# Small-head attentions: each stack of query and key pieces moved for 16 heads in one transfer, 18 transfers per batch in place of 36

## What is computed

```python
x = x + _L0_attn_a_ref(_layernorm(x), ...)   # here kind "norm": q and k get a layernorm over their 8 channels, no mask
x = x + _L0_ffn_ref(_layernorm(x), ...)      # six layers of local attention and MLP, run twice
x = x + _L0_attn_b_ref(_layernorm(x), ...)   # kind "latent": q, k, v through 32 latent channels, causal
...
x = x + _L1_attn_b_ref(_layernorm(x), ...)   # kind "plain": causal

logits = einsum('bhsd,bhtd->bhst', q, k) / sqrt(8)
att = softmax(logits)
out = einsum('bhst,bhtd->bhsd', att, v)      # then the 16 heads side by side, times a 128 x 128 matrix
```

## Time and profile before

| | |
|---|---|
| median of 3 runs | 4770.1 us (4769.83 to 4776.0) |
| the profiled execution | 4769.9 us, of which the span shown is 4768.1 us |
| PE busy | 4283.0 us (90%) |
| DVE, ACT, POOL busy | 3412.0, 2775.9, 2327.6 us |
| attention "norm" | about 35 to 375 us of the span |
| attention "latent" | about 2135 to 2430 us |
| attention "plain" | about 4398 to 4685 us |

### The profile page before, as it was taken

The page is one execution under the profiler, slowest core; times in us unless marked ns, Lnnn a source line. Parts: engine busy times, 40 slices in busy tenths (PEclk is TensorE's granted clock), DMA queues, the critical chain, the costliest instruction groups (busy, mean ns, idle before and its releaser), DMA issues. The chain is left out here.

```text
span 4768.1 us, 129948 instructions
## 1 busy us (share of the span) xinstructions
PE 4283.0 (90%) x54312; PEld 2101.0 (44%) x54312; DVE 3412.0 (72%) x5204; ACT 2775.9 (58%) x6997; POOL 2327.6 (49%) x1448
## 2 busy tenths in 40 slices
PE   5897999999999999976879999999999999877688
PEld 2222544544454544432434444454544444433343
DVE  3773888888888888853548888888888888733463
ACT  2664666666666666642546666666666666543354
POOL 3102766666666666642006666666666666500200
PEclk8998999999999999986889999999999999988699
DMA  5212000000000000003310000000000000000320
GB/s 150 32 19 58 2 20 7 2 20 7 20 7 20 7 2 2 2 4 41 41 37 24 2 23 3 20 6 20 7 2 24 2 2 2 2 4 9 49 33 10
DMA packets 87860, 88.62 MB, mean 19 GB/s; under 512 B 36632, under 2 KB 79860, under 8 KB 83444
## 3 DMA queue, kind: packets, MB, share of 16 engines
q1 hardware_dynamic: 86420, 74.11, 7.7%
q10 hardware_dynamic: 864, 6.29, 0.3%
HBM read 44.13 MB, written 7.34 MB: 11 GB/s over the span
## 5 line engine op out<-in xcount | busy, mean ns | idle before, releaser
L422 POOL TENSOR_TENSOR ra<-ra,rb 128x1024 f32<-128x1024 f32 x384 | 924.0, 2406 | 390.9 <-DVE rb L711 388.2
L436 POOL TENSOR_TENSOR qkr<-ra,inv 128x1024 f32<-128x1024 f32 x384 | 731.3, 1904 | 607.0 <-ACT inv L663 602.0
L466 PE MATMUL ps<-wvo,xs 128*32 128x512 f32 x6144 | 821.8, 607 | 72.6 <-ACT vs L599 52.3
L500 PE MATMUL ps<-wq,xs 128*128 128x512 f32 x1536 | 749.9, 611 | 19.5 <-DMA wq<-in_L_ffn_Wqkv 18.6
L641 ACT ACTIVATE pr<-ps,neg 128x64 f32<-128x64 f32 x3072 | 669.9, 338 | 0.6 <-DVE neg L688 0.6
L599 ACT ACTIVATE vs<-ps 128x512 f32<-128x512 f32 x768 | 451.7, 588 | 321.9 <-PE ps L466 320.2
L1428 DVE TENSOR_REDUCE nm<-ps 128x1 f32<-128x512 f32 (+3 forms) x768 | 382.1, 549 | 244.7 <-PE ps L1237 243.7
L688 DVE TENSOR_REDUCE neg<-ps 128x8 f32<-128x512 f32 x384 | 264.4, 688 | 379.7 <-PE ps L522 379.7
L652 ACT ACTIVATE inv<-ssq 128x16 f32<-128x16 f32 x384 | 82.8, 216 | 678.8 <-DVE ssq L746 678.8
L500 PEld LDWEIGHTS ps<-wq,xs 128*128 128x128 f32 x1536 | 273.4, 191 | 443.9 <-issue 352.3
L522 PEld LDWEIGHTS ps<-kt,qt 64*32 64x32 f32 x24576 | 359.5, 107 | 243.8 <-issue 243.8
(11 more groups left out here) (225 smaller groups left out, 6377.1 us busy)
## 6 DMA issues: line engine op xcount, KB each, us to landing
qs<-cut SPq DMA_DIRECT2D x216, 64.0 KB
ks<-cut SPq DMA_DIRECT2D x216, 64.0 KB
wq<-in_L_ffn_Wqkv SPq DMA_DIRECT2D x12, 1024.0 KB, 5.1
wvo<-wvo_scratch SPq DMA_DIRECT2D x12, 1024.0 KB, 4.9
wvo_scratch<-pt ACTq DMA_DIRECT2D x6, 1024.0 KB, 4.1
w<-in_L_ffn_W SPq DMA_DIRECT2D x12, 341.0 KB
pt<-in_L_ffn_Wqkv SPq DMA_DIRECT2D x6, 512.0 KB, 8.4
pt<-in_L_ffn_Wo SPq DMA_DIRECT2D x6, 512.0 KB, 7.7
```

Of the source, the lines that this page charges most:

```text
L422: pool.tensor_tensor(ra[:, m % 2, :, :], ra[:, m % 2, :, :], rb[:, :, :], ALU.add).then_inc(sum_done.sem, 1)
L436: pool.tensor_tensor(qkr[:, m % 2, :, :].rearrange("p s (h c) -> p (s h) c", c=HD), ra[:, m % 2, :, :].rearrange("p s (h c) -> p (s h) c", ...
L466: last = pe.matmul(VP[32 * j:32 * j + 32, :], xs[:, turn % 2, v * WIN:v * WIN + WIN], wvo[:, l % 2, j, :], start=True, stop=True)
L500: last = pe.matmul(PJ[:, qk, :], xs[:, turn % 2, t * P:t * P + P], wq[:, l % 2, at:at + 512], start=True, stop=True)
```

## The change

The order of channels becomes (channel, head) over all 128 partitions, so one DMA takes a piece for all 16 heads: from 128 partitions to 8, 128 KB in place of 64 KB. `ld_low` and `ld_high` become one `ld_stack`, for which PE waits at head 0. The transfers of batches 0 and 1 stand where the lower half stood (k = -15 and k = 1), those of batches 2 and 3 where the upper half stood (k = 16(b-1) + 7), behind the wait that the upper half had. The gamma and beta columns of "norm" are loaded by 4 DMAs in place of 8.

```diff
-        "mean_of_8": np.kron(np.eye(2), np.kron(np.full((SD, SD), 1 / SD), np.eye(SH // 2))).astype(np.float32),
+        "mean_of_8": np.kron(np.full((SD, SD), 1 / SD), np.eye(SH)).astype(np.float32),
...
                     for col, name in enumerate(("q_gamma", "q_beta", "k_gamma", "k_beta")):
-                        for e in range(2):
-                            by_row = d[f"{n}_{name}"][:, None].to_broadcast([SD, SH // 2])
-                            sp.dma_start(gb[P // 2 * e:P // 2 * e + P // 2, col:col + 1], by_row, allow_slow_non_contiguous=True).then_inc(ld_w.sem, 16)
+                        by_row = d[f"{n}_{name}"][:, None].to_broadcast([SD, SH])
+                        sp.dma_start(gb[:, col:col + 1], by_row, allow_slow_non_contiguous=True).then_inc(ld_w.sem, 16)
...
-            by_channel = lambda a: a.rearrange("p s (e c h) -> p s e h c", e=2, c=SD)
-            by_head = lambda a: a.rearrange("p s (e h c) -> p s e h c", e=2, c=SD)
-            n_ld = {"norm": 3 + 8 + 4, "latent": 7 + 4, "plain": 4}[kind]
+            by_channel = lambda a: a.rearrange("p s (c h) -> p s h c", c=SD)
+            by_head = lambda a: a.rearrange("p s (h c) -> p s h c", c=SD)
+            n_ld = {"norm": 3 + 4 + 4, "latent": 7 + 4, "plain": 4}[kind]
...
-            def stacks(b, low):
+            def stacks(b):
 
-                heads = slice(0, SH // 2) if low else slice(SH // 2, SH)
-                half = slice(0, P // 2) if low else slice(P // 2, P)
-                done = ld_low if low else ld_high
                 for part_ in range(PARTS):
                     sp.wait_ge(cut_done.sem, cut_done.at(5 * b + 2 * part_ + 1))
                     for to, s, p, c in [(qs, 0, c // PARTS, c) for c in range(PARTS * PARTS)] + [(ks, 1, c % PARTS, c) for c in range(PARTS * PARTS)]:
                         if p != part_:
                             continue
                         rows = slice(SD * c, SD * c + SD)
-                        sp.dma_start(to[rows, b % 2, heads, :], cut[half, p, s, :]).then_inc(done.sem, 16)
+                        sp.dma_start(to[rows, b % 2, :, :], cut[:, p, s, :]).then_inc(ld_stack.sem, 16)
...
-                if (b := batch_at(k, 1)) is not None:
-                    if b >= 2:
-                        sp.wait_ge(st_mm.sem, st_mm.at(NP * (SH * (b - 2) + SH // 2)))
-                    stacks(b, True)
-                if (b := batch_at(k, 7)) is not None:
+                if (b := batch_at(k, 1 if k < SH else 7)) is not None:
                     if b >= 2:
                         sp.wait_ge(st_mm.sem, st_mm.at(NP * SH * (b - 1)))
-                    stacks(b, False)
+                    stacks(b)
...
                     if b:
-                        pool.wait_ge(ld_low.sem, ld_low.at(16 * loads * b))
-                        pool.wait_ge(ld_high.sem, ld_high.at(16 * loads * b))
+                        pool.wait_ge(ld_stack.sem, ld_stack.at(16 * loads * b))
...
                 if n_ == 0 and h == 0:
-                    pe.wait_ge(ld_low.sem, ld_low.at(16 * loads * (b + 1)))
-                if n_ == 0 and h == SH // 2:
-                    pe.wait_ge(ld_high.sem, ld_high.at(16 * loads * (b + 1)))
+                    pe.wait_ge(ld_stack.sem, ld_stack.at(16 * loads * (b + 1)))
```

More of the change, by code:

```diff
@@ L929, in small_attention @@
     qk_normed, qk_ready, cut_done = ev("sa_qk_normed", "sa_qk_ready", "sa_cut_done")
-    ld_low, ld_high, *ld_m = ev("sa_ld_low", "sa_ld_high", "sa_ld_m_even", "sa_ld_m_odd")
+    ld_stack, *ld_m = ev("sa_ld_stack", "sa_ld_m_even", "sa_ld_m_odd")
     vw_turned, vw_made, vw_kept_act, vw_kept_dve, vw_out_act, vw_out_dve = ev(
@@ L1047, in _ @@
                     dve.tensor_tensor(by_channel(w[:, 0:2, :]), by_head(tmp[:, 0:2, :]),
-                                      mean.rearrange("p s (e h) -> p s e h", e=2)[:, :, :, :, None].to_broadcast([P, 2, 2, SH // 2, SD]), ALU.subtract).then_inc(prep_dve.sem, 1)
+                                      mean[:, :, :, None].to_broadcast([P, 2, SH, SD]), ALU.subtract).then_inc(prep_dve.sem, 1)
                     dve.tensor_copy(w[:, 2, :], tmp[:, 2, :])
@@ L1062, in _ @@
                     dve.wait_ge(prep_pe.sem, prep_pe.at(5))
-                    dve.tensor_copy(by_channel(w[:, 0:2, :]), ps[:, 0, 0:2 * P].rearrange("p (s e h c) -> p s e h c", s=2, e=2, c=SD))
+                    dve.tensor_copy(by_channel(w[:, 0:2, :]), ps[:, 0, 0:2 * P].rearrange("p (s h c) -> p s h c", s=2, c=SD))
                     dve.tensor_copy(w[:, 2, :], ps[:, 0, 2 * P:3 * P])
@@ L1498, in small_attention @@
     ones_set.past(1)
-    for e in (ld_low, ld_high):
-        e.past(16 * loads * BATCH)
+    ld_stack.past(16 * loads * BATCH)
     for e in ld_m:
```

## The result

The changed kernel takes **4969.9 us** (median of 4 runs, 4962.0 to 4972.1) against 4773.1 us (4 runs, 4769.8 to 4779.6) for the kernel before: **1.0408 times** as long, interval 1.039 to 1.0426. That is +197 us where +132 had been forecast: the sign and the mechanism were right, the size was short by a third, and the time lies only just inside the range. The profiled execution took 4962.0 us, its span is 4960.2 us, and against 4768.1 us before the span has grown by 192.1 us.

The account below looks back on a forecast made before the run. PE was taken to wait for maxima behind stack transfers draining by bytes. Later maxima +124.9, cold TensorE +10 and fewer gamma and beta loads -2.5 gave +132 us on 4769.9, so 4902 us; 8-in-10 range 4820 to 4970.

Parts of the forecast that it names:

- What bounds the place: Three small attentions: PE waits for maxima queued behind stack transfers, eleven waits, 79.5 us; bytes bound it, not transfer number.
- L: Time from first issue of a batch's stacks until all 2.36 MB have landed; taken as 36.5 us, bounds 31.1 and 38.0.
- rival 3: Stack sets drain worse than by bytes, at 53 GB/s: L 45.8 us, 5022 us; 4940 to 5030 given chance 0.10.
- Each us of L counts nine times: Batches 1 to 3 of three attentions each pay for L; 31.1 gives 4853 us, 38.0 gives 4916.
- 67 GB/s as the rate of the kernel before: Queued stacks drain at 67 GB/s; 100 GB/s appears in one of the twelve sets only.
- 124.9 as predicted: Later maxima in batches 1 to 3, in us: norm 47.9, latent 37.1, plain 39.9; together 124.9.
- cold TensorE: After a wait for maxima PE runs at a lower clock; five places newly waiting at 2.0 us each: +10.
- the loads of gamma and beta: Preparation of norm: four fewer issues of 0.62 us on SP, -2.5 us, bounds -2.5 and 0.
- The issue time: SP's issue of a batch 1 set still takes 11.8 us; even 23.6 us would cost nothing.
- Head 0's wait in latent: Batch 1: PE waits for the full stack, 17 us later, at no cost, covered by the wait for group 0's maxima.
- 1 (per transfer): Stack queue: 128 KB takes the 0.97 us of 64 KB, L 18.7 us, -68 us, 4702 us; 4700 to 4760 chance 0.08.
- 2 (100 GB/s, held back by issue alone): Stack queue keeps its fast state, 100 GB/s: L 24.9 us, 4769 us; chance 0.04.

Follow-up runs that it names:

- e6: The changed kernel with the three small maxima transfers issued by POOL on its own queue instead of SP's: 4843.9 us, 1.0146 of the kernel before.
- e1: The changed kernel with each stack transfer's 8 target partitions nine apart instead of neighbours: 4696.6 us, 0.9837 of the kernel before.
- e3: The kernel before with both 64 KB stacks put where the changed kernel has its one, transfer size unchanged: 4919.5 us, 1.0298 of the kernel before.
- e8: The changed kernel with its 18 transfers reordered, so 9 of 17 passages stay on the same partitions or those 32 away: 5003.1 us, 1.0478.
- e5: The changed kernel with each transfer's 8 target partitions two apart, the ninth pairing left as neighbours: 4798.5 us, 1.0055 of the kernel before.
- e2: The kernel before, with its 36 transfers of 64 KB, given target partitions nine apart: 4696.3 us, 0.9836 of the kernel before.
- e4: The changed kernel with the three small maxima transfers issued by ACT on its own queue instead of SP's: 4946.0 us, 1.0351 of the kernel before.

## Why the prediction was right in kind and short in size

**What bounds the place: right.** PE waits for the maxima behind the stacks. e6 moves the maxima to another queue and takes 126 us back; e1 leaves them there, makes the stacks drain, and takes back 273.

**L: the term that was mis-sized.** "By bytes, L is 2.36 MB / 67 GB/s" took the rate of the small transfer for that of the large one. Measured are 60 to 61 GB/s in five of the nine sets, 62 to 65 in the other four, and a mean L of 41.1 us. With the small transfers in the same places (e3) the mean L is the 36.5 us of the forecast, and the time 4919.5, 17 above it. So the 36.5 held for 64 KB and failed for 128 KB. Its likely cause was on the table as rival 3: the burst of about 100 GB/s once per transfer belongs to the passage between two transfers, and larger ones have half as many. The quarter-microsecond windows of the changed kernel in "latent":

```profile
2300.50:2300.75 0.25, 0.00 (x0) 0.00 (x0) 0.00 (x0) 0.00 (x0) 0.00 (x0) 0.50 0.54 57
2300.75:2301.00 0.25, 0.00 (x0) 0.00 (x0) 0.00 (x0) 0.00 (x0) 0.00 (x0) 0.50 0.49 78
2301.00:2301.25 0.25, 0.00 (x0) 0.00 (x0) 0.00 (x0) 0.00 (x0) 0.00 (x0) 0.50 0.72 86
2301.25:2301.50 0.25, 0.00 (x0) 0.00 (x0) 0.00 (x0) 0.00 (x0) 0.00 (x0) 0.50 0.55 53
```

This is the only burst among the twelve quarters from 2300 to 2303; before, the twelve from 2216 to 2219 have three, of 98 to 119 GB/s. e8 shows the passage at work. Rival 3 took the 53 GB/s for the whole set and put L at 45.8, as if the larger transfers had no burst at all. With its own mechanism, half as many bursts, the rows give the measured value: 0.97 us for the first 64 KB of a transfer and 64 KB / 53 GB/s = 1.24 us for the second, 18 times 2.21 and 1.3 us, an estimate of 41.0 us. I had given 4940 to 5030 us a chance of 0.10, with the alternation that speaks for it in the rows; it deserved more.

**Each us of L counts nine times: wrong, it counts eleven to twelve.** The forecast let batch 0's set stay as it was ("the same bytes"). But batch 0's set is one of the larger transfers too, and batch 1's cut hangs on its landing. It took 1.6 (norm), 4.7 (latent) and 10.6 us (plain) longer, measured on SP's and POOL's rows: 16.9 us. In plain the slip could be seen beforehand: batch 0's set stayed in the sum at its 31.1 us while every other set was given 36.5. Rival 3 counts the later landing of these sets (36 us), the main sum doesn't. From e5 to the changed kernel the sets of batch 0 grow by 1.6, 14.8 and 14.8 us, 2.2 for each of the 13.9 us of L, so that 11.2 of the 11.6 us are accounted for. The same quotient of the medians is 10.9 from e3 to the changed kernel and 10.7 from there to e8.

**67 GB/s as the rate of the kernel before: a reading that was too narrow.** The prediction held that the trace shows 100 GB/s in one of the twelve sets only. The set of batch 0 in "plain", the one of 31.1 us, drained faster as well. The windows of the kernel before:

```profile
4438.00:4440.00 2.00, 0.62 (x1) 0.00 (x0) 0.00 (x0) 0.60 (x1) 0.00 (x0) 0.50 0.57 90
4440.00:4442.00 2.00, 1.90 (x11) 1.46 (x12) 1.15 (x3) 0.00 (x0) 0.00 (x0) 0.50 0.57 91
```

Batch 1's in norm (79 to 111 GB/s from 114 to 128) and the upper stack of plain's batch 3 (79 to 90 from 4592 to 4604) did too, at a share of 0.54 to 0.60, with 64 KB transfers to neighbouring rows. In e3 the set of batch 0 in plain drains at 72 GB/s on the mean, where it was 82, and takes 35.2 us. So 4.1 of the 10.6 us came without the larger transfer. What lets such a set run faster stays open.

**Sum again.** 124.9 as predicted; 9 places by their own L less 36.5, +41.4; batch 0's sets, +16.9; cold TensorE, +10; the loads of gamma and beta, -4.8 (first stack of norm at 62.65 instead of 67.43, and 62.4 to 65.4 in the other kernels with that edit; predicted -2.5). That is 188.4 us of the 192.1 by which the span grew. With the 4.9 us between the attentions the sum is 1.2 us too large. The + 10 is the forecast's and was seen in two places only (below).

**Parts that held.** The issue time costs nothing: in latent each group of three from the fourth on took SP 3.4 to 7.4 us instead of 1.9, as the queue was full, and what lands last was behind the queue anyway. Head 0's wait in latent (21.64 us, expected 17) was covered as forecast: PE still waits another 25.18 us for the maxima afterwards. In plain it is 25.24 and in norm 9.22. The cold stretch is there: from the landing to the next group's cut 9.5 us (238.76 to 248.2) and 9.7 (333.71 to 343.4), where 7.8 stood without a wait.

**Rivals.** 1 (per transfer) is refuted by the result itself, L being 41.1 us and not 18.7, and by e1, where a transfer of 128 KB takes less than the 0.97 us. 2 (100 GB/s, held back by issue alone) wasn't met in any set that counted: in none of the nine did the rate come near 100. A stretch of norm's batch 0 does show 102 GB/s after, where it had 100 before; why stays open.

**Why neighbours are slow.** Measured with 128 KB transfers, by where 8 partitions lie: 60 to 65 GB/s side by side, 98 to 102 two apart, 157 to 182 nine apart, at nearly the same DMA share, 0.52 to 0.57 in the windows shown. The Trainium skill ("SBUF — State Buffer", Door 1: The DMA port swizzle) says that bandwidth goes by the number of 16 ports reached, four neighbouring partitions to a port and the ones 32 further on to the same. By it the three layouts reach two, four (the ninth pairing two) and eight ports, which by its figures is an estimate of 54, 109 and 218 GB/s. The traces have the order and, for the first two, nearly the size; for the third they have less than the estimate, where the rate is near the 200 GB/s at which SP issues (128 KB per 0.656 us). e8's order puts transfers on the same ports behind one another, and comes to 56 to 59, the nearest to 54. The excess over 54 in the changed kernel would then be two neighbours in the queue working on different ports for a moment. That reading fits e3, e8 and the quarters, but it doesn't say why some sets before kept about 90 GB/s; no run measured it directly.

## What to carry to other kernels

Before transfers are merged or moved, ask what drains their queue. If the rate goes by where the bytes land, a larger transfer gains nothing and can lose, and the cure is to spread the target partitions (here one line, -1.6%, and -2.2% with the set a few steps later). Ask next which small transfer stands behind them and how soon it is needed; put it on the queue of an engine that idles (126 us back here), not of the one that feeds the bottleneck (24 us back). And when a duration is multiplied in a sum, look for every place it enters, the ones that "don't change" first.

## What the runs showed of the hardware that was not expected

- It matters which eight partitions are the target: 60 to 65 GB/s as neighbours, about 100 two apart, up to 182 at a distance of nine, with the DMA share nearly unchanged at some 0.55. The share does not tell how well the queue drains.
- Doubling a transfer from 64 to 128 KB raised the mean L from 36.5 to 41.1 us where the targets were neighbours (e3 and the changed kernel), and did nothing to the time where they were spread (e2 and e1).
- A second queue is only in part a way round a full first one. In e4, ACT's timeline has the issue and PE's the matmul that waited:

```profile
2272.64 1.81 ACTq L1379 DMA_DIRECT2D qs<-mcut  x3
```

```profile
2286.38 0.29 PE L1236 MATMUL ps<-ident,cmask 128*128 128x128 bf16 x1 [8.47 <-DMA qs<-mcut]
```

  It takes 13.7 us until the last of three transfers of 4 KB has landed, beside SP's full queue; where no stack is in flight it takes 2.9 to 3.0 us.
- SP's issue is held back by what is queued: in latent each of the 128 KB transfers from the thirteenth on took 2.0 to 2.5 us to issue instead of 0.64 (6.47 us for three, rows above). The maxima behind batch 1's set were so issued at 2291.52, where 18 times 0.64 us would give an estimate of 2280.
